# A perceiver block on one core: attended values projected in three rounded terms, key norms' powers asked for between filter taps, one product of constants moved

## The reference

```
x = x + xattn(layernorm(x), ctx)      # softmax((ctx Wg + bg) x^T) over the context, times ctx, then @ Wo + bo
x = x + delta(layernorm(x))           # 4 heads of 128
    q, k, v = silu(short_conv(h @ W)) # causal, 4 taps; beta = sigmoid(h @ Wb)
    delta_out = delta rule over chunks of 32, with q and k divided by their norms
    local = fir(v) with 3, 15 and 63 taps
    o = softmax gates of (local x 3, delta_out, v); rmsnorm(o) @ Wo.T
x = x + moe(layernorm(x))             # top 2 of 8 experts and 2 shared ones, 512 wide
```

## Time and profile before

| | us |
|---|---|
| three runs | 440.35, 436.7, 437.32 (median 437.32) |
| the profiled execution, its own time | 441.51 |
| its span in the trace | 439.3 |
| PE busy, matmuls | 425.7 (97%) |
| DVE, ACT, POOL busy | 316.9, 183.4, 78.7 |

### The profile page before, as it was taken

The page is one execution under the profiler, slowest core; times in us unless marked ns, Lnnn a source line. Parts: engine busy times, 40 slices in busy tenths (PEclk is TensorE's granted clock), DMA queues, the critical chain, the costliest instruction groups (busy, mean ns, idle before and its releaser), DMA issues.

```text
span 439.3 us, 8275 instructions
## 1 busy us (share of the span) xinstructions
PE 425.7 (97%) x3218; PEld 295.8 (67%) x3218; DVE 316.9 (72%) x582; ACT 183.4 (42%) x245; POOL 78.7 (18%) x78
## 2 busy tenths in 40 slices
PE   6999999999999999999999999999999999999996
PEld 4953335744445757688766488888887888888872
DVE  4642235698889898896747967594478899999965
ACT  1102111487753211023134155434418788887730
POOL 1000000000023610226651000074600000000061
PEclk9999999999998999999969999999999999999999
DMA  7999989736302441057000200067489999999545
GB/s 257 435 428 423 427 342 354 242 91 189 108 12 104 116 133 27 2 188 295 1 1 0 82 16 2 0 225 266 157 300 404 353 360 401 374 389 403 202 136 169
DMA packets 18226, 92.43 MB, mean 210 GB/s; under 512 B 3456, under 2 KB 5264, under 8 KB 11152
## 3 DMA queue, kind: packets, MB, share of 16 engines
q1 hardware_dynamic: 15168, 78.82, 47.3%
q10 hardware_dynamic: 1488, 8.93, 5.8%
q0 software_dynamic: 1536, 4.20, 2.9%
HBM read 82.25 MB, written 12.08 MB: 215 GB/s over the span
## 4 chain that ended last, share of the span: by engine, by line
PE 82%; DVE 9%; DMA 3%; SPq 2%; issue 1%; ACT 1%; POOL 1%; DVEq 0%; ACTq 0%
PE bank L963 33%; PE bank L777 9%; PE bank L702 6%; PE bank L728 4%; PE bank L560 4%; PE bank L610 3%; PE bank L631 3%; PE bank L587 3%; SPq L368 2%; PE bank L753 2%; PE bank L939 2%; DMA early<-wffn_in 1%; DVE part L1559 1%; PE bank L754 1%; DVE x L1775 1%
## 5 line engine op out<-in xcount | busy, mean ns | idle before, releaser
L1559 DVE SCALAR_TENSOR_TENSOR part<-ring,cols,part 128x504 f32<-128x504 f32 (+13 forms) x64 | 41.9, 713 | 0.1
L777 PEld LDWEIGHTS bank<-ring 64*64 64x64 f32 x960 | 33.4, 140 | 10.6 <-issue 9.2
L777 PE MATMUL bank<-ring 64*64 64x64 f32 (+1 forms) x960 | 37.9, 231 | 1.3 <-issue 1.0
L728 PE MATMUL bank<-xnT,ring 128*128 128x512 f32 (+1 forms) x96 | 37.7, 544 | 0.7 <-ACT xnT L1123 0.7
L463 POOL TENSOR_TENSOR small<-small 128x1 f32<-128x1 f32 (+2 forms) x12 | 12.0, 1004 | 133.3 <-DVE small L1436 72.0
L702 PE MATMUL bank<-early,ring 128*32 128x512 f32 (+15 forms) x512 | 33.3, 402 | 0.0
L1559 DVE SCALAR_TENSOR_TENSOR ring<-bank,cols,ring 128x504 f32<-128x504 f32 (+2 forms) x36 | 26.3, 733 | 5.1 <-ACT ring L1170 4.1
L728 PEld LDWEIGHTS bank<-xnT,ring 128*128 128x128 f32 x96 | 17.6, 190 | 17.1 <-issue 14.5
L702 PEld LDWEIGHTS bank<-early,ring 128*32 128x32 f32 x512 | 14.5, 112 | 14.9 <-issue 11.2
L472 POOL TENSOR_TENSOR ring<-ring,consts 128x256 f32<-128x256 f32 x20 | 15.8, 812 | 47.0 <-DVE ring L1691 32.7
L1303 ACT ACTIVATE rows<-bank 128x512 f32<-128x512 f32 x19 | 11.4, 598 | 30.6 <-PE bank L963 26.7
(11 more groups left out here) (272 smaller groups left out, 948.7 us busy)
## 6 DMA issues: line engine op xcount, KB each, us to landing
early<-wffn_in SPq DMA_DIRECT2D x19, 1024.0 KB, 7.8
ring<-ctxT_in SPq DMA_DIRECT2D x4, 2048.0 KB, 20.7
ring<-ctx_in SPq DMA_DIRECT2D x4, 2048.0 KB, 34.9
raw1b<-wffn_in SPq DMA_DIRECT2D x7, 1024.0 KB
raw3b<-wffn_in SPq DMA_DIRECT2D x7, 1024.0 KB
raw2b<-wffn_in SPq DMA_DIRECT2D x6, 1024.0 KB, 7.7
ring<-firw_in SPq DMA_DIRECT2D x4, 1024.0 KB, 5.2
xs<-zeros_in ACTq DMA_DIRECT2D x1, 3840.0 KB, 14.0
```

The source lines that it names most:

```text
L728: last = pe.matmul(bank[QB[g % 3]][:, ts], wqkv[:, j, c, h * P:(h + 1) * P], xnT[:, c, ts], start=(c == 0), stop=(c == DC - 1))
L777: last = pe.matmul(dst[s, d], left[s, L * t:L * (t + 1)], right(s, t), start=True, stop=True)
L1559: return dve.scalar_tensor_tensor(out=d, in0=s, scalar=w, in1=d, op0=ALU.mult, op1=ALU.add)
```

## The change

Four things change; no work is taken out, and none is given to another core or queue.

1. `project` works on rounded halves. ScalarE writes the high part of the turned values (`high_values`) and, once, the high part of the weights (`high_projection`, 128 x 2048); VectorE subtracts them to get the low parts, in place of its copy. `project` then makes 12 fp32r matmuls of three terms where it made 4 fp32 ones. Its waits are on the high parts first, and on the low ones from the second term on.
2. `want_powers(0)` stands after tap 12 (not 16), the taps ahead of `table_low` end at 18 (not 20), and the first two entries of `tap_ends` change so that the first two updates have 8 and 3 taps ahead of them (not 7 and 2).
3. On PE one of three filter rounds ahead of the key factors, and the first of the six that follow them, now stand between the factors of heads 1 and 2.
4. The product of constants of step 9 is gone, and one stands at step 6, after `square_sums(0)`.

```
-                pe.wait_ge(S["oT_ready"], t + 1)
-                pe.wait_ge(ld_wox, 16)
+                pe.wait_ge(S["o_kept"], max(O_HI[t], WOX_HI))
...
-                for c in range(DC):
-                    last = pe.matmul(bank[2 + t % 2][:, :], oT_b[:, t % 2, c * P:(c + 1) * P], wox[:, c, :],
-                                     start=(c == 0), stop=(c == DC - 1))
+                for n, (values_of, w, low) in enumerate(((oT_hi, wox_hi, 0), (oT_lo, wox_hi, O_LO[t]),
+                                                         (oT_hi, wox_lo, max(O_LO[t], WOX_LO)))):
+                    if low:
+                        pe.wait_ge(S["oT_ready"], low)
+                    for c in range(DC):
+                        last = pe.matmul(bank[2 + t % 2][:, :], values_of[t][:, c * P:(c + 1) * P], w[:, c, :],
+                                         start=(n == 0 and c == 0), stop=(n == 2 and c == DC - 1))
...
-            fir_rounds(0, 7, 10)
+            fir_rounds(0, 7, 9)
             pe.wait_ge(S["ct_lo"], 1)
             pe.wait_ge(S["conv_done"], 3 * H - 2)
-            for h in range(H):
-                key_factor(h)
+            key_factor(0)
+            key_factor(1)
+            fir_rounds(0, 9, 11)
+            key_factor(2)
+            key_factor(3)
...
-            fir_rounds(0, 10, FW)
+            fir_rounds(0, 11, FW)
...
                 if step == 6:
                     square_sums(0, 6)
+                    pe.wait_ge(S["o_ready"], 2)
+                    keep_warm(bank[7][:, :], 1)
...
                 if step < 8:
                     weights_spread(step)
-                else:
-                    pe.wait_ge(S["o_ready"], 2)
+                if step == 8:
                     keep_warm(bank[7][:, :], 1)
...
+            def high_values(t):
+                act.wait_ge(S["oT_done"], t + 1)
+                if t >= 2:
+                    act.wait_ge(S["proj_done"], t)
+                act.activation(oT_hi[t], bank[4][:, :], ACT.Copy).then_inc(S["o_kept"], 1)
+
+            def high_projection():
+                act.wait_ge(S["y_done"], NT)
+                act.wait_ge(ld_wox, 16)
+                act.activation(wox_hi, wox, ACT.Copy).then_inc(S["o_kept"], 1)
...
-                dve.tensor_copy(oT_b[:, t % 2, :], bank[4][:, :]).then_inc(S["oT_ready"], 1)
+                dve.wait_ge(S["o_kept"], O_HI[t])
+                dve.tensor_tensor(oT_lo[t], bank[4][:, :], oT_hi[t].bitcast(F32),
+                                  ALU.subtract).then_inc(S["oT_ready"], 1)
...
+                if t == 0:
+                    dve.wait_ge(S["o_kept"], WOX_HI)
+                    dve.tensor_tensor(wox_lo, wox, wox_hi.bitcast(F32), ALU.subtract).then_inc(S["oT_ready"], 1)
...
-            tap_ends = (20, 27, 29, 33, 38, 42, 46, 50, 55, 59, all_taps)
+            tap_ends = (18, 26, 29, 33, 38, 42, 46, 50, 55, 59, all_taps)
```

More of the change, by code:

```diff
@@ L108, in perceiver_block @@
             ring = sb("ring", [P, 4, 8192], held=before)
+            with ExitStack() as over_part:
+                part_r = sb("part_r", [P, 3, 4, 512], F32R, held=over_part)
             part = sb("part", [P, 3, 4, 512], held=before)
@@ L152, in perceiver_block @@
         probsT_b = early[:, 1, 1024:2048].rearrange("p (i n) -> p i n", i=2)
-        oT_b = early[:, 2, 0:1024].rearrange("p (i n) -> p i n", i=2)
+        wox_hi, wox_lo = part_r[:, 0], part_r[:, 1]
+        oT_hi, oT_lo = ([part_r[:, 2, 2 * min(t, 1) + i, :] for t in range(NT)] for i in range(2))
+        O_KEPT, O_HI, WOX_HI = (1, 4, 6, 8), (2, 5, 7, 9), 3
+        O_LO, WOX_LO = (1, 3, 4, 5), 2
         o_b = early[:, 2, 1024:2048].rearrange("p (i n) -> p i n", i=2)
@@ L544, in transpose_tile @@
                 elif layer == 1:
-                    pe.wait_ge(S["o_kept"], NT)
+                    pe.wait_ge(S["o_kept"], O_KEPT[NT - 1])
                     pe.wait_ge(S["pT_ready"], NT)
@@ L606, in values @@
                 else:
-                    pe.wait_ge(S["o_kept"], t - 1)
+                    pe.wait_ge(S["o_kept"], O_KEPT[t - 2])
                 for k in range(TK // P):
@@ L615, in turn_values @@
             def turn_values(t):
-                pe.wait_ge(S["o_kept"], t + 1)
+                pe.wait_ge(S["o_kept"], O_KEPT[t])
                 if t >= 1:
-                    pe.wait_ge(S["oT_ready"], t)
+                    pe.wait_ge(S["oT_ready"], O_LO[t - 1])
                 for c in range(DC):
@@ L1141, in _ @@
                 act.activation(probsT_b[:, t % 2, :], bank[7][:, :], ACT.Copy).then_inc(S["pT_ready"], 1)
+                if t >= 1:
+                    high_values(t - 1)
                 if t < NT - 1:
                     exponentials(t + 1)
+                if t == 1:
+                    high_projection()
                 act.wait_ge(S["pv_done"], t + 1)
@@ L1149, in _ @@
                                scale=rsm[:, t:t + 1]).then_inc(S["o_kept"], 1)
+            high_values(NT - 1)
             act.dma_start(xs[0:MAXB * P], zeros_in).then_inc(zeroed, 16)
@@ L1500, in _ @@
                     score_bias(t + 2)
-                dve.wait_ge(S["oT_done"], t + 1)
-                if t >= 2:
-                    dve.wait_ge(S["proj_done"], t - 1)
-                dve.tensor_copy(oT_b[:, t % 2, :], bank[4][:, :]).then_inc(S["oT_ready"], 1)
+                dve.wait_ge(S["o_kept"], O_HI[t])
+                dve.tensor_tensor(oT_lo[t], bank[4][:, :], oT_hi[t].bitcast(F32),
+                                  ALU.subtract).then_inc(S["oT_ready"], 1)
                 if t + 2 < NT:
                     normalise(t + 2)
+                if t == 0:
+                    dve.wait_ge(S["o_kept"], WOX_HI)
+                    dve.tensor_tensor(wox_lo, wox, wox_hi.bitcast(F32), ALU.subtract).then_inc(S["oT_ready"], 1)
                 if t >= 2:
@@ L1670, in _ @@
             gating_3()
-            fir_taps(8, 16)
+            fir_taps(8, 12)
             want_powers(0)
             convolve(2 * H + 1)
+            fir_taps(12, 14)
             key_table()
-            fir_taps(16, 17)
             convolve(2 * H + 2)
-            fir_taps(17, 20)
+            fir_taps(14, 18)
             table_low(0, ct_k, 3)
```

## The result

Over 22 executions of each, the changed kernel took **436.12 us** in the median (432.96 to 439.14), the kernel before 439.62 (435.11 to 442.12). The ratio is **0.9944**, 95% interval 0.9921 to 0.9967: faster by 0.56%, which is 2.5 us and about half of the 5.2 us that the forecast of 434.4 stands under 439.6 (the medians alone lie 3.5 apart). A ratio here leaves out executions over 1.5% above a kernel's fastest and isn't the quotient of the two medians. The time lies in the predicted range. The profiled execution took 435.51 us, with a span of 433.6.

A forecast was written before the change was run, and what follows sets the result against it. TensorE's order of work was taken as the bound. From the profiled 441.5: -2.9 - 0.1 - 0.5 + 0.9 - 3.8 - 0.8 gave 434.3; from the fastest run, 434.6; forecast 434.4 us, range 431.8 to 438.4.

The forecast's parts named there:

- Projection, -2.9: Cross-attention: twelve fp32r matmuls replace four fp32 ones in each of four projections, saving 2.8 to 3.2 us, taken as 2.9.
- The first projection's cover: First projection at 46.86: the weights' low part is ready by 48.5, needed at 48.7, so it costs 0 to 0.2 us.
- hidden, by 0.4: Last projection: ScalarE's delayed DMA issues still let the turned tile's store end by 71.3, before the projection's end at 71.7.
- Key norms, -0.1: Keys' table and solve: 0.75 us gained by asking earlier, 0.66 given back at the solve; from -0.8 to +0.5.
- the third tap: Second update of the solve: one more tap ahead of it costs 0.66 us, though 1.2 was possible.
- the wait of 0.39: First level of the solve: TensorE waits 0.39 us for VectorE's second update, so a tap added there isn't covered.
- Clock between the factors, -0.5: Stretch from 135.7 to 139.0 us: filter rounds in the gaps may keep the clock up, gaining 0.5 us on the profiled execution.
- Product of constants, -3.7: Last level: the product moved to step 6 costs 0.9 us, holding the clock gains 3.8, dropping step 9's gains 0.8.
- the +0.9: Step 6 of the last level: the added product of constants costs 0.9 us, with TensorE as the bound.
- The slower rival: Last level to `solved`: step 9's removed product was what kept the clock, so 4.6 us are lost, 439.2; chance 0.08.
- The sum: Whole kernel: all terms added take the profiled execution from 441.5 to 434.3 us.

The follow-up runs named there:

- e12: The kernel after with the three zero transfers issued behind `high_values(2)`, right after the high part of tile 2; 440.31 us, 0.9921 of before.
- e1: The kernel before with the three-term projection alone; 442.21 us, 1.0072 of before.
- e7: The kernel before with its three zero transfers issued later, behind the stores of turned tiles 0 and 1; 445.74 us, 1.0157 of before.
- e8: The kernel before with the three-term projection alone and the zero transfers ahead of the last tile's high part; 438.09 us, 0.9947 of before.
- e3: The kernel after with the three zero transfers issued ahead of the last tile's high part; 433.25 us, 0.9889 of before, and again 432.44 us, 0.9893.
- r2: The kernel after, unchanged, measured again on the chip of the last four experiments; 435.48 us, 0.9950 of before.
- e6: The kernel before with only the key norms' moved powers and taps and the filter rounds between the factors; 440.72 us, 1.0021 of before.
- e9: The kernel after with the three zero transfers issued by SyncE behind the last filter's stack copies; 434.91 us, 0.9912 of before.
- r1: The kernel after, unchanged, measured again on the chip of the first zero-transfer tests; 436.99 us, 0.9928 of before.
- e11: The kernel before with the three-term projection alone and the zero transfers issued by SyncE behind the last stack copies; 438.99 us, 0.9985 of before.
- e2: The kernel after with only the projection change undone; 435.51 us, 0.9920 of before.
- e5: The kernel after without the product of constants at step 6 of the last level; 440.19 us, 1.0000 of before.
- e4: The kernel before with only the product of constants moved from step 9 to step 6; 436.79 us, 0.9956 of before.
- e10: The kernel before with the three zero transfers issued by SyncE behind the last filter's stack copies; 439.58 us, 1.0007 of before.

## Why the prediction was wrong, and what of it held

**Projection, -2.9: the term right, its place in the sum wrong.** It measured -2.79 to -2.83 in every trace that has it except e12's, where the late weights stand in the same stretch. The first projection's cover held as worked out. The step that failed is the one sentence that called ScalarE's three DMA issues "hidden, by 0.4". It asked only whether ScalarE would be late for the store of the turned tile (it wasn't: the store ended at 70.32, 0.36 us ahead of the projection's end), and never what the transfers themselves would meet: SyncE's stack copies. Those are released by TensorE's progress and came 2.8 us earlier, while the zeros, now behind the last high part, came 2.0 later. The lead of the zeros' first issue over the first copy shrank from 21.7 us to 16.8. e1, e7, e8, and e3 beside r2, show it. The price in the kernel after is 3.0 us by the medians and 2.5 by the ratios, which is about what the measured gain falls short: e3 has the forecast's change, 0.989 where 434.4 beside 439.6 is 0.988.

**Key norms, -0.1: mis-sized, and it mattered otherwise than stated.** e6 alone has -0.66 at the keys' table, -1.48 at the first transpositions and -0.82 when the first queries' table is turned, so the third tap gives back 0.66 as forecast and 0.8 is kept. About half of that belongs to the next term, the clock: from the keys' table to the first transpositions e3, at full clock between the factors, gains 0.81, and e9, whose clock fell there, 0.39. What is left for the norms is some -0.4, inside the stated -0.8 to +0.5. The earlier trace rows name no releaser for the wait of 0.39 ("issue"); that it was for VectorE's update, as the prediction has it, fits the update's end at 155.71, 0.1 us ahead of the product. More important is what the term wasn't priced for: with VectorE late, moving four taps behind the asking is worth far more. At the keys' table e1 is 0.37 late, the kernel after 1.98 early (1.21 in r1, 1.35 in r2). Without late copies the same taps are worth 0.24 there (e11 3.22 early, e9 3.46).

**Clock between the factors, -0.5.** Where it held, it was worth 0.42, the difference of e3 and e9 above. It held in the profiles of after, e2, both of e3, e5 and e6; in r1, r2 and e9 that window reads 0.83, in e12 0.93. Without the moved rounds it reads 0.83 or 0.84 in before, e1, e4, e7, e10 and e11, but 1.00 in e8. So the rounds help in a part of the executions, and aren't all that decides.

**Product of constants, -3.7.** From `square_sums(0, 6)` to the output projection, e4 gains 4.67 us on before's profile, after 4.67 and e3 4.66, and e2, r1, r2 and e9 the same. Of the forecast's terms the +0.9 was right (0.97); the gains were 1.0 too small together. The slower rival, that the product of step 9 kept the clock, is refuted by these seven.

**The sum** of the profiled pair should have been -7.2 (441.5 to 434.3) and was -6.0: 441.5 to 435.5. Of these, 1.1 came from a start that happened to be earlier. Counted from the second turn, the kernel after stands 1.98 us ahead at the keys' table, 0.54 at `square_sums(0, 6)` (the fall at 202 us took 1.3), 5.21 at the output projection and 4.6 at the end of the span. e3 stands 3.45, 3.61, 8.27 and 7.8 ahead, in its second profile 8.0 at the end: with the zeros out of the way the forecast's 7.2 are passed. The 8.27 are the measured terms, 2.8 + 0.4 + 0.4 + 4.7, and 0.3 to 0.5 of them is lost again in the experts. The forecast's other error was in the reference. I took 437.3, the median of three runs, for a kernel without slow stretches, and the profiled 441.5 for one with two. Over 22 to 35 executions on each chip before's median is 438.5 to 440.2, and its median clock 0.984 on three chips and 0.992 on one: the falls are the rule. That made the same 434.4 a change of 0.7% by the one reading and 1.2% by the other; the runs gave 0.56%.

## What to carry on

Work saved on one engine arrives at the end only if the next wait on the way doesn't take it: follow the engine to its next wait and see what releases that one, and on which schedule. A DMA issue that is pushed back by a few instructions has to be checked against every transfer that starts while it is in flight; moving three issues here was worth as much as the change itself, and 3.6 us further ahead lost it again in seven executions of twelve. And where the granted clock differs between executions, take its spread from many runs before pricing an edit that steadies it.

The best kernel of these runs is **e3**: the change, with the zeros issued ahead of the last high part, 432.4 to 433.3 us, 0.989 of before.

## What was not expected of the hardware

A DMA issue can hold its queue. Of SyncE's sixteen issues of 590 ns each, one took 4311 ns in the kernel after, while the zeros issued by ScalarE (3840 and 2560 KB) were landing; with these transfers 3.4 us earlier or far away (e3, e9) the sixteen took 10.2 to 10.7 us in all. In the kernel after it ended 0.4 us before the second of these transfers had landed. The traces show the coincidence and e7 the dependence, not which part of the DMA path was full.

In e1 and e7 TensorE came out of a single wait of 3.77 and 3.54 us at the low clock, and in r1 out of one of 2.20: its next eight records took 4.83 us for 3.60. After 2.04 us in r2, 1.93 in e8 and 1.44 in after they took 3.60. In e1 the low clock took another 2.6 us by the first spread, on top of the 3.2 that the wait had cost.
